# Experts by couples of pairs, with the rest rows of the second product in four quarters of TensorE's array

## The chip, the cores and the metric

The kernel runs on one core of a Trainium2 chip. The metric is the device time of one execution in microseconds (us). TensorE does the matrix products and writes to PSUM banks; VectorE and ScalarE read PSUM; GpSimd (POOL) issues gathers; SyncE (SP) issues the other DMAs. The engines run beside each other and meet at semaphores.

## The reference, cut to what matters

Two layers of a network on 256 tokens of width 512: cross-attention on a context of 4096 rows, self-attention and a feed-forward part, then attention with memory, self-attention and a mixture of experts. The change touches only the last part, the mixture of experts:

```python
logits = x @ router_w.T                      # 256 tokens, 64 experts
wts, idx = top_k(softmax(logits), 8)         # 8 experts a token, weights normalised
# each expert gets up to C = 64 of its tokens (slots)
h = silu(einsum('ecd,efd->ecf', xg, w1)) * einsum('ecd,efd->ecf', xg, v1)    # F = 192
y = einsum('ecf,efd->ecd', h, w2)            # D = 512
out = zeros(T, D).at[tok].add(y[e, slot] * weight)
```

The first products are [64 slots x 512] by [512 x 384] (w1 and v1 side by side), the second [64 x 192] by [192 x 512], for each of 64 experts. All of it is in float32.

## The kernel before, in words

Experts go by pairs: 32 pairs of 2 experts of 64 slots, so that a pair has 128 slot rows. The part begins when the tokens are routed, at about 1477 us. For a pair p:

- `up(p)` (L1912): for each of 4 chunks of the width, one product for each expert, with 64 stationary columns, that writes to its half of the partitions of a bank; the two use the array's column halves (L1924). 384 moving columns each.
- ScalarE applies Silu (L2028). `make_hid` (L2068) on VectorE multiplies by the other half and by the gate weight, into `h`: one instruction for hidden rows 0 to 127 and two for the rest, rows 128 to 191 (`REST` = 64), which go to different column blocks for the two experts, beside zeros.
- `turn(p)` (L1929): two transposes of `h` into `TURN_B`; `move_hid` (L2085) copies 256 columns to `hidT`.
- `down(p)` (L1938): two half-array products with hidden rows 0 to 127 of each expert (L1944), then one of the full array (L1945). Its 128 contraction rows are rows 128 to 191 of the first expert and rows 128 to 191 of the second; each expert's slots see zeros where the other's rows are.
- `round_y` on ScalarE (L2004) and `split_y` on VectorE (L2091) make a rounded part and a remainder of y. `make_selT` (L2058) makes a 0/1 matrix from slots to tokens.
- `spread_out(p)` (L1947): four products that add y into the 256 tokens' sums in two banks (L1953).

The order on TensorE is written out by hand: up(p), every fourth time `find_gates` (L1888, L41), `turn_rows(p+1)` (L1905, L1909), down(p-1), spread_out(p-2), turn(p). ScalarE and VectorE follow the same order with their parts. For pairs from 4 on, the tokens' rows are gathered from DRAM by POOL (`gpsimd_rows`, L1849), as soon as `move_gates` (L2047) has written the group's indices, into four buffers that `turn_rows` frees; a group is 4 pairs.

The weights of a pair are one DMA of 2304 KB (`w_moe`), issued by SP. There are 7 buffers (`N_RING`). The first 7 loads are issued at 1402 to 1406 us (L1855). Load p goes out when `down(p-7)` is finished:

```python
for p in range(N_RING, PAIRS):
    e.wait_ge(hid_down, p - N_RING + 1)
    e.dma_start(ring[p % N_RING][:], a["w_moe"][p]).then_inc(moe_in[p % N_RING], 16)
```

Of the kernel before, what the change touches and what calls it, by code (L numbers as in the profile page):

```python
# [6 lines left out]
F32 = mybir.dt.float32  # L7
# [3 lines left out]
ALU = mybir.AluOpType  # L11
# [3 lines left out]
P = 128  # L15
T, D = 256, 512
# [47 lines left out]
def build(nc, a, out):  # L64
    ctx = ExitStack()
    with ctx:
# [35 lines left out]

        IDENT_SET, ATT_SET, LOW_ONES, MASKS_SET, SLOTS_COUNTED, SLOTS_SET, H_ZEROED, IDS_COUNTED, IDS_SET = 4, (8, 9), 10, 12, 15, 17, 18, 19, 20

# [1657 lines left out]
        def gpsimd_memory(e):  # L1762
# [6 lines left out]
        N_RING, EPP, GROUP, FIRST, N_ROWS = 7, 2, 4, 4, 4  # L1769
        NG = PAIRS // GROUP  # L1770
        UPW = DT * 2 * FF
        W2 = EPP * UPW
# [9 lines left out]
            ("rows6", [P, N_ROWS, D], F32), ("xgT", [P, 2, DT, P], F32),  # L1782
            ("sa", [P, 2, FF], F32), ("h", [P, 2, 2 * P], F32), ("hidT", [P, 2, 2 * P], F32), ("gs", [P, 2, GROUP], F32),
            ("y_hi", [P, 2, D], F32R), ("y_lo", [P, 2, D], F32R), ("selT", [P, 2, T], F32R),
# [34 lines left out]
        PART = 3 * EPP  # L1819

        def gpsimd_slots(e):

            e.memset(low[:], 1.0).then_inc(consts_set, 1)
            e.memset(ones_m[:], 1.0).then_inc(consts_set, 1)
            e.wait_ge(consts_set, LOW_ONES)
            e.affine_select(out=low[:], in_=low[:], compare_op=ALU.is_gt, fill=0.0, base=0,
                            pattern=[[1, P]], channel_multiplier=-1).then_inc(consts_set, 1)
            e.iota(slot_row_i[:], pattern=[[1, CAP]], base=1, channel_multiplier=0).then_inc(consts_set, 1)
            for n, rows in enumerate(halves):
                e.wait_ge(consts_set, MASKS_SET + n + 1)  # L1830
                e.iota(slot_col_i[rows], pattern=[[0, 1]], base=1, channel_multiplier=1).then_inc(consts_set, 1)
            e.wait_ge(consts_set, SLOTS_COUNTED)
            e.tensor_copy(slot_row[:], slot_row_i[:]).then_inc(consts_set, 1)
            e.tensor_copy(slot_col[:], slot_col_i[:]).then_inc(consts_set, 1)
            e.memset(h[:], 0.0).then_inc(consts_set, 1)
            e.iota(ids_i[:], pattern=[[P, TT], [0, PAIRS], [0, EPP]], base=0, channel_multiplier=1).then_inc(consts_set, 1)
            e.wait_ge(consts_set, IDS_COUNTED)
            e.tensor_copy(gate_parts[:, :, :, 2 * EPP:], ids_i[:]).then_inc(consts_set, 1)
# [20 lines left out]
        def sync_moe(e):  # L1859
# [11 lines left out]
            for p in range(N_RING, PAIRS):  # L1871
                e.wait_ge(hid_down, p - N_RING + 1)
                e.dma_start(ring[p % N_RING][:], a["w_moe"][p]).then_inc(moe_in[p % N_RING], 16)
# [5 lines left out]
        def tensor_moe(e):  # L1879
# [8 lines left out]
            def find_gates(g):  # L1888

                e.wait_ge(sel_made, TT * (g + 1))  # L1890
                if g == 0:
                    e.wait_ge(route_gate, TT)
                    e.wait_ge(slot_moved, 1)
                    e.wait_ge(consts_set, IDS_SET)
                else:
                    e.wait_ge(gates_moved, 3 * g)
                    if g > 1:
                        e.wait_ge(hid_moved, GROUP * (g - 1))
                for n in range(GROUP):
                    pair = slice(n * P, (n + 1) * P)  # L1900
                    t = matmuls(e, TURN_B[:, 2 * P + PART * n:2 * P + PART * (n + 1)],
                                [(sel[:, g % 2, i, pair], gate_parts[:, i, GROUP * g + n, :]) for i in range(TT)])
                t.then_inc(gates_found, 1)

            def turn_rows(p):  # L1905
                e.wait_ge(*rows_landed(p))
                e.wait_ge(xg_moved, DT + p - GROUP)
                for c in range(DT):
                    t = e.transpose(GATHER_B[:, c * P:(c + 1) * P], rows6[:, p % N_ROWS, c * P:(c + 1) * P], ident[:])  # L1909
                t.then_inc(rows_turned, 1)  # L1910

            def up(p):  # L1912
                g, n = divmod(p, GROUP)
                e.wait_ge(moe_in[p % N_RING], 16 * (p // N_RING + 1))
                if p >= 2:
                    e.wait_ge(hid_made, 3 * (p - 1))
                if p >= GROUP:
# [10 lines left out]

            def turn(p):  # L1929
                e.wait_ge(hid_made, 3 * (p + 1))  # L1930
                if p:
                    e.wait_ge(hid_moved, p)
                e.wait_ge(gates_moved, 3 * min(p // GROUP + 2, NG))
                for n in range(2):
                    t = e.transpose(TURN_B[:, n * P:(n + 1) * P], h[:, p % 2, n * P:(n + 1) * P], ident[:])
                t.then_inc(hid_turned, 1)

            def down(p):  # L1938
                w2 = ring[p % N_RING]
                e.wait_ge(hid_moved, p + 1)  # L1940
                if p >= 2:
                    e.wait_ge(y_split, p - 1)
                for s, rows in enumerate(halves):
                    e.matmul(banks[Y_BANK[p % 2]][rows], hidT[:, p % 2, rows], w2[:, W2 + s * D:W2 + (s + 1) * D], start=True, stop=False)  # L1944
                e.matmul(banks[Y_BANK[p % 2]][:], hidT[:, p % 2, P:2 * P], w2[:, W2 + 2 * D:], start=False, stop=True).then_inc(hid_down, 1)  # L1945

# [30 lines left out]
            find_gates(0)  # L1977
            for p in range(PAIRS + 2):
                g, n = divmod(p, GROUP)
                if p < PAIRS:  # L1980
                    up(p)
                if n == 0 and g + 1 < NG:
                    find_gates(g + 1)
                if GROUP <= p + 1 < PAIRS:
                    turn_rows(p + 1)
                if 1 <= p <= PAIRS:
                    down(p - 1)
                if p >= 2:
                    spread_out(p - 2)
                if p < PAIRS:  # L1990
                    turn(p)

        def scalar_moe(e):
# [10 lines left out]
            def round_y(p):  # L2004
                e.wait_ge(hid_down, p + 1)
                if p >= 2:
# [13 lines left out]
            for c in range(DT):  # L2020
                move_xg(c)
            for p in range(PAIRS + 1):
                g, n = divmod(p, GROUP)
                if p < PAIRS:
                    e.wait_ge(hid_up, p + 1)
                    if p >= 2:
                        e.wait_ge(hid_made, 3 * (p - 1))
                    e.activation(sa[:, p % 2, :], banks[UP_BANKS[p % 2]][:, 0:FF], ACT.Silu).then_inc(hid_silu, 1)  # L2028
                if GROUP <= p + 1 < PAIRS:
                    move_rows(p + 1)  # L2030
                if p:
                    round_y(p - 1)

        def vector_moe(e):
# [12 lines left out]
            def move_gates(g):  # L2047
                e.wait_ge(gates_found, g + 1)
                if g >= 2:
                    e.wait_ge(hid_made, 3 * GROUP * (g - 1))  # L2050
                if g >= 3:
                    e.wait_ge(rows_turned, GROUP * (g - 2))
                found = TURN_B[:, 2 * P:2 * P + PART * GROUP].rearrange("p (n k) -> p n k", k=PART)
                e.tensor_copy(ids[:, g % 2, :], found[:, :, 2 * EPP]).then_inc(gates_moved, 1)
# [13 lines left out]
            def make_hid(p):  # L2068
# [3 lines left out]
                if n == 0:  # L2072
                    e.wait_ge(gates_moved, 3 * (g + 1))
                if p == 0:
                    e.wait_ge(consts_set, H_ZEROED)
                if p >= 2:
                    e.wait_ge(hid_turned, p - 1)
                e.wait_ge(hid_silu, p + 1)
                e.scalar_tensor_tensor(h[:, p % 2, 0:P], up_b[:, FF:FF + P], gs[:, g % 2, n:n + 1], sa[:, p % 2, 0:P],
                                       ALU.mult, ALU.mult).then_inc(hid_made, 1)  # L2080
                for s, rows in enumerate(halves):
                    e.scalar_tensor_tensor(h[rows, p % 2, P + s * REST:P + (s + 1) * REST], up_b[rows, FF + P:2 * FF],
                                           gs[rows, g % 2, n:n + 1], sa[rows, p % 2, P:FF], ALU.mult, ALU.mult).then_inc(hid_made, 1)

            def move_hid(p):  # L2085
                e.wait_ge(hid_turned, p + 1)
                if p >= 2:
                    e.wait_ge(hid_down, p - 1)
                e.tensor_copy(hidT[:, p % 2, :], TURN_B[:, 0:2 * P]).then_inc(hid_moved, 1)

# [40 lines left out]
            make_sel(1)  # L2131
            for p in range(PAIRS + 1):
                g, n = divmod(p, GROUP)
                if p < PAIRS:
                    make_hid(p)
                if n == 0 and g + 1 < NG:
                    move_gates(g + 1)
                if p:
                    split_y(p - 1)
                if p < PAIRS:  # L2140
                    move_hid(p)
                    if n == 1 and g + 2 < NG:
                        make_sel(g + 2)
                    make_selT(p)
            e.wait_ge(spread, PAIRS)
# [102 lines left out]
```

## Time and profile before

| | |
|---|---|
| median of 3 runs | 1696.14 us (1693.32 to 1700.35) |
| the profiled execution | 1698.13 us, its span 1696.3 us |
| TensorE's mean granted clock | 0.992 |
| busy: PE / PEld / DVE / ACT / POOL | 97% / 76% / 64% / 41% / 7% of the span |
| HBM read and written | 200.69 MB and 68.19 MB |
| weight loads of the experts | 32 of 2304 KB |

PE is TensorE's matmuls, PEld its loads of the stationary operand, DVE is VectorE, ACT ScalarE. The time of an execution is a little more than the span from its first to its last instruction. Lines such as L1945 are lines of the kernel before. One float32 matmul of the program stands in the trace as two MATMUL instructions.

### The profile page before, as it was taken

The page shows a single profiled execution, that of the slowest core. Times are in us where ns is not written, and L with a number is a line of the kernel's source. Part 1 is how long each engine was busy: PE and PEld are TensorE (multiplying, and loading weights), DVE is VectorE, ACT ScalarE, POOL GpSimd, SP SyncE. Part 2 cuts the span into 40 slices and gives each one's busy share as a digit, 9 for nine tenths or more (in the row PEclk, how much of TensorE's full clock was granted, in tenths as well). Part 3 has the DMA queues.
Part 4 walks back from the last instruction along what each step waited for, and adds up shares of the span by engine and source line. Part 5 has one row for each costly group of instructions (what it writes and reads, how often), then busy time and mean ns, then how long its engine had stood idle before and what let it go on. Part 6 is the DMA issues. An engine that isn't in the chain of part 4 may idle for free.

```text
span 1696.3 us, 23514 instructions
## 1 busy us (share of the span) xinstructions
PE 1651.4 (97%) x9232; PEld 1296.9 (76%) x9232; DVE 1089.0 (64%) x1754; ACT 696.2 (41%) x938; POOL 127.0 (7%) x213
## 2 busy tenths in 40 slices
PE   8998999999999999999999999998899999999998
PEld 7887888888788888888888888887657646644444
DVE  4445777777767777677777779997544923633333
ACT  3334444454444444445454456564321312222221
POOL 0000000000000000000000011101000000111110
PEclk9999999999999999999999999999889999999999
DMA  6755454455455445545545453326110529199991
GB/s 223 207 173 154 131 133 134 119 137 131 137 137 136 128 120 134 149 119 142 131 127 136 117 143 100 103 91 211 76 50 1 198 71 423 50 386 395 398 383 43
DMA packets 117293, 270.41 MB, mean 159 GB/s; under 512 B 7168, under 2 KB 76992, under 8 KB 111040
## 3 DMA queue, kind: packets, MB, share of 16 engines
q1 hardware_dynamic: 96512, 194.45, 36.5%
q0 software_dynamic: 20672, 74.46, 14.9%
q8 instruction: 74, 1.21, 0.3%
q14 instruction: 35, 0.29, 0.1%
HBM read 200.69 MB, written 68.19 MB: 159 GB/s over the span
## 4 chain that ended last, share of the span: by engine, by line
PE 77%; issue 11%; DVE 5%; DMA 3%; ACT 2%; POOL 1%; SPq 0%; DVEq 0%; POOLq 0%; ACTq 0%
PE bank L390 18%; PE bank L41 17%; PE bank L362 14%; PE bank L403 7%; PE bank L1924 5%; PE bank L1554 3%; PE bank L1945 2%; PE bank L1944 2%; DMA v_dram<-v_out 2%; PE bank L1953 2%; PE bank L135 2%; PE bank L428 1%; PE bank L1909 1%; DVE e_lo L719 1%; DMA v_out<-in_wv 1%
## 5 line engine op out<-in xcount | busy, mean ns | idle before, releaser
L719 DVE TENSOR_TENSOR e_lo<-S,e_hi 128x1024 fp32r<-128x1024 f32 x128 | 156.6, 1224 | 90.3 <-ACT e_hi L548 89.8
L362 PE MATMUL bank<-cT_hi,wk_hi 128*128 128x512 f32 x512 | 205.4, 401 | 0.0
L390 PE MATMUL bank<-wv_hi,cT_hi 128*128 128x512 f32 x512 | 200.0, 391 | 3.5 <-DVE wv_lo L656 3.5
L539 ACT ACTIVATE S<-S 128x1024 f32<-128x1024 f32 x128 | 135.8, 1061 | 158.5 <-DVE S L699 158.0
L362 PE MATMUL bank<-cT_hi,wk_lo 128*128 128x512 f32 x512 | 200.5, 392 | 0.0
L390 PE MATMUL bank<-wv_hi,cT_lo 128*128 128x512 f32 x512 | 199.4, 389 | 0.0
L390 PE MATMUL bank<-wv_lo,cT_hi 128*128 128x512 f32 x512 | 199.2, 389 | 0.0
L362 PE MATMUL bank<-cT_lo,wk_hi 128*128 128x512 f32 x512 | 199.2, 389 | 0.0
L548 ACT CAST e_hi<-S 128x1024 fp32r<-128x1024 f32 x128 | 134.8, 1053 | 141.3 <-PE bank L403 136.7
L712 DVE TENSOR_TENSOR esum<-esum,S 128x512 f32<-128x512 f32 x210 | 145.0, 690 | 71.2 <-ACT S L539 67.6
L403 PE MATMUL bank<-e_hi,v_back 128*128 128x256 f32 x880 | 168.5, 289 | 6.3 <-DVE e_lo L719 3.9
L687 DVE TENSOR_TENSOR mx<-mx,S 128x512 f32<-128x512 f32 x224 | 154.3, 689 | 14.3 <-ACT S L533 10.4
L699 DVE TENSOR_TENSOR S<-S,mrow 128x1024 f32<-128x1024 f32 x128 | 155.4, 1216 | 3.2 <-POOL mrow L896 3.2
L41 PE MATMUL bank<-q_hi,k_hi 128*128 128x256 f32 x512 | 145.3, 284 | 9.3 <-DVE k_lo L674 9.3
L403 PEld LDWEIGHTS bank<-e_hi,v_back 128*128 128x128 f32 x880 | 139.5, 193 | 11.2 <-DMA v_back<-v_dram 5.1
L41 PE MATMUL bank<-q_lo,k_hi 128*128 128x256 f32 x512 | 144.8, 283 | 0.0
L41 PE MATMUL bank<-q_hi,k_lo 128*128 128x256 f32 x512 | 144.8, 283 | 0.0
L519 ACT CAST k_hi<-bank 128x512 fp32r<-128x512 f32 x128 | 75.3, 588 | 155.3 <-PE bank L362 155.3
L533 ACT COPY S<-bank 128x1024 f32<-128x1024 f32 x128 | 128.7, 1006 | 11.1 <-PE bank L41 11.1
L403 PE MATMUL bank<-e_lo,v_back 128*128 128x256 f32 x440 | 124.9, 284 | 0.0
L890 POOL DMA_DIRECT2D v_back<-v_dram x110 | 59.0, 537 | 870.2 <-PE bank L403 833.9
L724 DVE TENSOR_TENSOR v_out<-bank,v_out 128x512 fp32r<-128x512 f32 x112 | 76.9, 687 | 60.3 <-ACT v_out L555 60.3
(280 smaller groups left out, 2872.2 us busy)
## 6 DMA issues: line engine op xcount, KB each, us to landing
w<-in_w_moe SPq DMA_DIRECT2D x32, 2304.0 KB, 11.6
v_dram<-v_out SPq DMA_DIRECT2D x112, 512.0 KB, 4.5
v_back<-v_dram POOLq DMA_DIRECT2D x110, 512.0 KB, 5.0
v_dram<-v_back SPq DMA_DIRECT2D x16, 512.0 KB, 3.9
ctx_nat<-in_ctx SPq DMA_DIRECT2D x8, 1024.0 KB, 5.2
ctx_raw<-in_ctxT SPq DMA_DIRECT2D x7, 1024.0 KB, 7.8
v_late<-v_dram POOLq DMA_DIRECT2D x14, 512.0 KB, 3.6
l_w_qkv<-in_l_wqkv SPq DMA_DIRECT2D x6, 1024.0 KB, 5.6
```

Source lines behind the costliest of these rows:

```text
L41: last = e.matmul(dst, lhs, rhs, start=(n == 0), stop=(n == len(terms) - 1))
L362: t = e.matmul(banks[b][:], l, r, start=(c == 0 and m == 0), stop=(c == DT - 1 and m == 2))
L390: t = e.matmul(banks[b][:], l, r, start=(c == 0 and m == 0), stop=(c == DT - 1 and m == 2))
L403: t = e.matmul(banks[O_BANK][:, 0:T], v[:, i, l, :], r[:, i, :], start=(j == 0 and i == 0 and m == 0), stop=(j == NCH - 1 and i == CT - 1 ...
L533: e.copy(S[:, j * CT:(j + 1) * CT, :].rearrange("p a t -> p (a t)"), twin[:]).then_inc(s_stored, 1)
L539: e.activation(Sj, Sj, ACT.Exp).then_inc(raised, 1)
L548: e.copy(e_place(n)[0][:], S[:, j * CT:(j + 1) * CT, :]).then_inc(e_rounded, 1)
L687: own.done(e.tensor_tensor(mx[:], mx[:], two, ALU.max))
L699: e.tensor_tensor(Sj, Sj, mrow[:].unsqueeze(1).to_broadcast([P, CT, T]), ALU.subtract).then_inc(shifted, 1)
L712: e.tensor_tensor(esum[:], esum[:], two, ALU.add).then_inc(e_summed, 1)
L719: e.tensor_tensor(lo[:], Sj, hi[:].bitcast(F32), ALU.subtract).then_inc(e_split, 1)
L1924: t = e.matmul(banks[UP_BANKS[p % 2]][rows, 0:2 * FF], inputs[:, s * P // 2:(s + 1) * P // 2], ring[p % N_RING][:, s * UPW + c * 2 * FF:s ...
```

## The change

Two pairs, a couple, go through each step together: 16 couples q of pairs 2q and 2q+1. The order on TensorE is up(2q), on every second couple find_gates, up(2q+1), turn_rows(2q+2), down of couple q-1, spread_out of both pairs of couple q-2, turn(q), turn_rows(2q+3).

`h` has 384 columns: 128 main columns of the first pair, 128 of the second, then 64 rest columns of the first and 64 of the second. The two experts of a pair share columns now, so that no zeros are needed, and one transpose puts the first pair's rest rows on partitions 0 to 63 and the second pair's on 64 to 127. In `down`, the four main products come first, then four products of 64 contraction rows and 64 stationary columns, one for each quarter of the array: rows of the array by pair, columns by expert; each pair adds to its own bank. The host lays the rest of `w2` out to fit. The loads' sizes stay the same. SP waits for whole couples: loads p = 2q+5 and 2q+6 need `down` of couple q-1. The gates of groups from 1 on are found in `GATHER_B`, which `turn_rows` uses too, and not in `TURN_B`.

```diff
+            return (TURN_B[:, 2 * P:2 * P + PART * GROUP] if g == 0 else GATHER_B[:, 0:PART * GROUP]).rearrange("p (n k) -> p n k", k=PART)
...
-            e.memset(h[:], 0.0).then_inc(consts_set, 1)
...
-                e.wait_ge(hid_down, p - N_RING + 1)
+                e.wait_ge(hid_down, (p - N_RING) // 2 + 1)
...
+                if p % GROUP == 2 and p // GROUP + 1 < NG:
+                    e.wait_ge(gates_moved, 3 * (p // GROUP + 2))
...
+            def turn(q):
+
+                e.wait_ge(hid_made, 4 * (q + 1))
+                if q:
+                    e.wait_ge(hid_moved, q)
+                else:
+                    e.wait_ge(gates_moved, 3)
+                for n in range(3):
+                    t = e.transpose(TURN_B[:, n * P:(n + 1) * P], h[:, n * P:(n + 1) * P], ident[:])
+                t.then_inc(hid_turned, 1)
+
+            def down(q):
+
+                e.wait_ge(hid_moved, q + 1)
+                if q:
+                    e.wait_ge(y_split, 2 * q)
+                ring_of = [ring[(2 * q + n) % N_RING] for n in range(2)]
                 for n in range(2):
-                    t = e.transpose(TURN_B[:, n * P:(n + 1) * P], h[:, p % 2, n * P:(n + 1) * P], ident[:])
-                t.then_inc(hid_turned, 1)
-
-            def down(p):
-                w2 = ring[p % N_RING]
-                e.wait_ge(hid_moved, p + 1)
-                if p >= 2:
-                    e.wait_ge(y_split, p - 1)
+                    for s, rows in enumerate(halves):
+                        e.matmul(banks[Y_BANK[n]][rows], hidT[:, n * P + s * P // 2:n * P + (s + 1) * P // 2],
+                                 ring_of[n][:, W2 + s * D:W2 + (s + 1) * D], start=True, stop=False)
                 for s, rows in enumerate(halves):
-                    e.matmul(banks[Y_BANK[p % 2]][rows], hidT[:, p % 2, rows], w2[:, W2 + s * D:W2 + (s + 1) * D], start=True, stop=False)
-                e.matmul(banks[Y_BANK[p % 2]][:], hidT[:, p % 2, P:2 * P], w2[:, W2 + 2 * D:], start=False, stop=True).then_inc(hid_down, 1)
+                    for n, rest in enumerate(halves):
+                        t = e.matmul(banks[Y_BANK[n]][rows], hidT[rest, 2 * P + s * P // 2:2 * P + (s + 1) * P // 2],
+                                     ring_of[s][rest, W2 + 2 * D:], start=False, stop=True)
+                t.then_inc(hid_down, 1)
...
+            for q in range(COUPLES + 2):
+                if q < COUPLES:
+                    up(2 * q)
+                    if q % 2 == 0 and q // 2 + 1 < NG:
+                        find_gates(q // 2 + 1)
+                    up(2 * q + 1)
+                if GROUP <= 2 * q + 2 < PAIRS:
+                    turn_rows(2 * q + 2)
+                if 1 <= q <= COUPLES:
+                    down(q - 1)
+                if q >= 2:
+                    spread_out(2 * q - 4)
+                    spread_out(2 * q - 3)
+                if q < COUPLES:
+                    turn(q)
+                if GROUP <= 2 * q + 3 < PAIRS:
+                    turn_rows(2 * q + 3)
...
-                for s, rows in enumerate(halves):
-                    e.scalar_tensor_tensor(h[rows, p % 2, P + s * REST:P + (s + 1) * REST], up_b[rows, FF + P:2 * FF],
-                                           gs[rows, g % 2, n:n + 1], sa[rows, p % 2, P:FF], ALU.mult, ALU.mult).then_inc(hid_made, 1)
...
+                e.scalar_tensor_tensor(h[:, rest:rest + REST], up_b[:, FF + P:2 * FF], gs[:, g % 2, n:n + 1], sa[:, p % 2, P:FF],
+                                       ALU.mult, ALU.mult).then_inc(hid_made, 1)
+
+            def move_hid(q):
+                e.wait_ge(hid_turned, q + 1)
+                if q:
+                    e.wait_ge(hid_down, q)
+                e.tensor_copy(hidT[:], TURN_B[:, 0:3 * P]).then_inc(hid_moved, 1)
...
+            for q in range(COUPLES + 1):
+                if q < COUPLES:
+                    if q % 2 == 0 and q // 2 + 1 < NG:
+                        move_gates(q // 2 + 1)
+                    make_hid(2 * q)
+                    make_hid(2 * q + 1)
+                if q:
+                    for p in (2 * q - 2, 2 * q - 1):
+                        split_y(p)
+                        make_selT(p)
+                if q < COUPLES:
+                    move_hid(q)
+                    if q % 2 and q // 2 + 2 < NG:
+                        make_sel(q // 2 + 2)
```

## Rows read from the trace of the kernel before

**Rows 1.** Busy time by stretches: PE, PEld, DVE, ACT, POOL, clock, DMA, GB/s.
```profile
1500.00:1656.00 156.00, 156.00 (x790) 74.96 (x788) 57.30 (x168) 34.61 (x69) 22.77 (x24) 1.00 0.99 398
1500.00:1530.00 30.00, 30.00 (x158) 14.45 (x155) 10.57 (x32) 6.35 (x13) 3.80 (x4) 1.00 1.01 427
...
1560.00:1600.00 40.00, 40.00 (x201) 18.91 (x201) 15.45 (x43) 9.03 (x18) 6.64 (x7) 1.00 0.98 375
```

**Rows 2.** Chain of waits, pairs 4 and 5: start us, us, what.
```profile
1499.65 2.73 PE bank L1924 x16
1502.38 0.98 PE bank L41 x8
1503.37 0.52 PE bank L1909 x4
1503.88 1.01 PE bank L1944 x4
1504.89 1.06 PE bank L1945 x2
1505.95 0.92 PE bank L1953 x4
...
1507.09 2.73 PE bank L1924 x16
1509.82 0.59 PE bank L1909 x4
...
1513.62 0.47 PE bank L1924
```

**Rows 3.** Chain of waits at the start of the expert part.
```profile
1477.35 2.75 PE bank L1924 x16
...
1482.06 0.41 PE bank L1935 x2
...
1485.20 0.86 PE bank L1944 x4
```

**Rows 4.** Chain of waits from the last pair's first products on.
```profile
1681.35 2.73 PE bank L1924 x16
...
1691.27 1.21 PE bank L1953 x4
```

**Rows 5.** Chain of waits in self-attention, then that line's instructions by shape.
```profile
1430.51 0.43 PE bank L1062 x8
...
L1062 PE MATMUL bank<-l_qkT x64: 372/374/478, 1429.7 to 1450.3; 32*128 32x256 f32 x64
```

**Rows 6.** Weight loads: issue and landing of two, landing of the last.
```profile
L1873 SPq DMA_DIRECT2D w<-in_w_moe x1: 339/339/339, 1492.0 to 1492.0; - x1
...
DMA to landing us min/median/max: 14.4/14.4/14.4
...
L1873 SPq DMA_DIRECT2D w<-in_w_moe x1: 328/328/328, 1525.6 to 1525.6; - x1
...
DMA to landing us min/median/max: 11.2/11.2/11.2
...
DMA to landing us min/median/max: 12.2/12.2/12.2
```

**Rows 7.** Groups of 1476 to 1697 us on ScalarE and VectorE: busy, mean ns, idle.
```profile
L2095 DVE TENSOR_TENSOR y_lo<-bank,y_hi 128x512 fp32r<-128x512 f32 x32 | 22.1, 692 | 64.0 <-ACT y_hi L2008 64.0
L2008 ACT CAST y_hi<-bank 128x512 fp32r<-128x512 f32 x32 | 18.8, 586 | 49.4 <-PE bank L1945 49.4
...
L2089 DVE COPY hidT<-bank 128x256 f32<-128x256 f32 x32 | 13.3, 415 | 0.6 <-PE bank L1935 0.6
...
L2066 DVE TENSOR_SCALAR selT<-slot_all,slot_col 128x256 fp32r<-128x256 bf16 x32 | 11.1, 345 | 0.0
```

**Rows 8.** Gathers of token rows: issues and landings of all 28.
```profile
L1849 POOL DMA_INDIRECT rows<-xn_dram,ids x28: 947/947/1189, 1483.0 to 1652.3; - x28
...
DMA to landing us min/median/max: 4.1/8.9/13.3
```

More of the change, by code:

```diff
@@ L100, in build @@
         own = Steps(vector_step)
-        IDENT_SET, ATT_SET, LOW_ONES, MASKS_SET, SLOTS_COUNTED, SLOTS_SET, H_ZEROED, IDS_COUNTED, IDS_SET = 4, (8, 9), 10, 12, 15, 17, 18, 19, 20
+        IDENT_SET, ATT_SET, LOW_ONES, MASKS_SET, SLOTS_COUNTED, SLOTS_SET, IDS_COUNTED, IDS_SET = 4, (8, 9), 10, 12, 15, 17, 18, 19
         def gpsimd_constants(e):
@@ L1770, in build @@
         NG = PAIRS // GROUP
+        COUPLES = PAIRS // 2
         UPW = DT * 2 * FF
@@ L1782, in build @@
             ("rows6", [P, N_ROWS, D], F32), ("xgT", [P, 2, DT, P], F32),
-            ("sa", [P, 2, FF], F32), ("h", [P, 2, 2 * P], F32), ("hidT", [P, 2, 2 * P], F32), ("gs", [P, 2, GROUP], F32),
+            ("sa", [P, 2, FF], F32), ("h", [P, 3 * P], F32), ("hidT", [P, 3 * P], F32), ("gs", [P, 2, GROUP], F32),
             ("y_hi", [P, 2, D], F32R), ("y_lo", [P, 2, D], F32R), ("selT", [P, 2, T], F32R),
@@ L1819, in build, with gates_place @@
         PART = 3 * EPP
+        def gates_place(g):
+            return (TURN_B[:, 2 * P:2 * P + PART * GROUP] if g == 0 else GATHER_B[:, 0:PART * GROUP]).rearrange("p (n k) -> p n k", k=PART)
         def gpsimd_slots(e):
@@ L1896, in find_gates @@
                     e.wait_ge(gates_moved, 3 * g)
-                    if g > 1:
-                        e.wait_ge(hid_moved, GROUP * (g - 1))
+                    e.wait_ge(xg_moved, DT + GROUP * (g - 2) + 2 if g > 1 else DT)
                 for n in range(GROUP):
                     pair = slice(n * P, (n + 1) * P)
-                    t = matmuls(e, TURN_B[:, 2 * P + PART * n:2 * P + PART * (n + 1)],
+                    t = matmuls(e, gates_place(g)[:, n, :],
                                 [(sel[:, g % 2, i, pair], gate_parts[:, i, GROUP * g + n, :]) for i in range(TT)])
@@ L1915, in up @@
                 if p >= 2:
-                    e.wait_ge(hid_made, 3 * (p - 1))
+                    e.wait_ge(hid_made, 2 * (p - 1))
                 if p >= GROUP:
@@ L1927, in up @@
                 t.then_inc(hid_up, 1)
[L1929 to L1933, printed above, removed]
-                for n in range(2):
-                    t = e.transpose(TURN_B[:, n * P:(n + 1) * P], h[:, p % 2, n * P:(n + 1) * P], ident[:])
-                t.then_inc(hid_turned, 1)
-            def down(p):
-                w2 = ring[p % N_RING]
-                e.wait_ge(hid_moved, p + 1)
-                if p >= 2:
-                    e.wait_ge(y_split, p - 1)
+            def turn(q):
[12 more added lines that the diff above has]
+                ring_of = [ring[(2 * q + n) % N_RING] for n in range(2)]
+                for n in range(2):
+                    for s, rows in enumerate(halves):
+                        e.matmul(banks[Y_BANK[n]][rows], hidT[:, n * P + s * P // 2:n * P + (s + 1) * P // 2],
+                                 ring_of[n][:, W2 + s * D:W2 + (s + 1) * D], start=True, stop=False)
                 for s, rows in enumerate(halves):
-                    e.matmul(banks[Y_BANK[p % 2]][rows], hidT[:, p % 2, rows], w2[:, W2 + s * D:W2 + (s + 1) * D], start=True, stop=False)
-                e.matmul(banks[Y_BANK[p % 2]][:], hidT[:, p % 2, P:2 * P], w2[:, W2 + 2 * D:], start=False, stop=True).then_inc(hid_down, 1)
+                    for n, rest in enumerate(halves):
+                        t = e.matmul(banks[Y_BANK[n]][rows], hidT[rest, 2 * P + s * P // 2:2 * P + (s + 1) * P // 2],
+                                     ring_of[s][rest, W2 + 2 * D:], start=False, stop=True)
+                t.then_inc(hid_down, 1)
             def spread_out(p):
@@ L1977, in tensor_moe @@
             find_gates(0)
[L1978 to L1991, printed above, removed]
+            for q in range(COUPLES + 2):
[15 more added lines that the diff above has]
+                    turn_rows(2 * q + 3)
         def scalar_moe(e):
@@ L2004, in round_y @@
             def round_y(p):
-                e.wait_ge(hid_down, p + 1)
+                e.wait_ge(hid_down, p // 2 + 1)
                 if p >= 2:
@@ L2021, in scalar_moe @@
                 move_xg(c)
[L2022 to L2032, printed above, removed]
+            for q in range(COUPLES + 1):
+                if q < COUPLES:
+                    for p in (2 * q, 2 * q + 1):
+                        e.wait_ge(hid_up, p + 1)
+                        if p >= 2:
+                            e.wait_ge(hid_made, 2 * (p - 1))
+                        e.activation(sa[:, p % 2, :], banks[UP_BANKS[p % 2]][:, 0:FF], ACT.Silu).then_inc(hid_silu, 1)
+                if GROUP <= 2 * q + 2 < PAIRS:
+                    move_rows(2 * q + 2)
+                if q:
+                    round_y(2 * q - 2)
+                    round_y(2 * q - 1)
+                if GROUP <= 2 * q + 3 < PAIRS:
+                    move_rows(2 * q + 3)
         def vector_moe(e):
@@ L2049, in move_gates @@
                 if g >= 2:
-                    e.wait_ge(hid_made, 3 * GROUP * (g - 1))
+                    e.wait_ge(hid_made, 2 * GROUP * (g - 1))
                 if g >= 3:
                     e.wait_ge(rows_turned, GROUP * (g - 2))
-                found = TURN_B[:, 2 * P:2 * P + PART * GROUP].rearrange("p (n k) -> p n k", k=PART)
+                found = gates_place(g)
                 e.tensor_copy(ids[:, g % 2, :], found[:, :, 2 * EPP]).then_inc(gates_moved, 1)
@@ L2073, in make_hid @@
                     e.wait_ge(gates_moved, 3 * (g + 1))
-                if p == 0:
-                    e.wait_ge(consts_set, H_ZEROED)
                 if p >= 2:
-                    e.wait_ge(hid_turned, p - 1)
+                    e.wait_ge(hid_turned, p // 2)
                 e.wait_ge(hid_silu, p + 1)
-                e.scalar_tensor_tensor(h[:, p % 2, 0:P], up_b[:, FF:FF + P], gs[:, g % 2, n:n + 1], sa[:, p % 2, 0:P],
+                main, rest = p % 2 * P, 2 * P + p % 2 * REST
+                e.scalar_tensor_tensor(h[:, main:main + P], up_b[:, FF:FF + P], gs[:, g % 2, n:n + 1], sa[:, p % 2, 0:P],
                                        ALU.mult, ALU.mult).then_inc(hid_made, 1)
-                for s, rows in enumerate(halves):
-                    e.scalar_tensor_tensor(h[rows, p % 2, P + s * REST:P + (s + 1) * REST], up_b[rows, FF + P:2 * FF],
-                                           gs[rows, g % 2, n:n + 1], sa[rows, p % 2, P:FF], ALU.mult, ALU.mult).then_inc(hid_made, 1)
[L2085 to L2089, printed above, removed]
+                e.scalar_tensor_tensor(h[:, rest:rest + REST], up_b[:, FF + P:2 * FF], gs[:, g % 2, n:n + 1], sa[:, p % 2, P:FF],
[5 more added lines that the diff above has]
+                e.tensor_copy(hidT[:], TURN_B[:, 0:3 * P]).then_inc(hid_moved, 1)
             def split_y(p):
@@ L2131, in vector_moe @@
             make_sel(1)
[L2132 to L2144, printed above, removed]
+            for q in range(COUPLES + 1):
+                if q < COUPLES:
[3 more added lines that the diff above has]
+                    make_hid(2 * q + 1)
+                if q:
+                    for p in (2 * q - 2, 2 * q - 1):
+                        split_y(p)
+                        make_selT(p)
+                if q < COUPLES:
+                    move_hid(q)
+                    if q % 2 and q // 2 + 2 < NG:
+                        make_sel(q // 2 + 2)
             e.wait_ge(spread, PAIRS)
@@ L2221 @@
     w2_main = w2[:, :P].reshape(PAIRS, 2, P, D).transpose(0, 2, 1, 3)
-    moe = (up.reshape(PAIRS, P, -1), w2_main.reshape(PAIRS, P, -1), w2[:, P:].reshape(PAIRS, P, D))
+    moe = (up.reshape(PAIRS, P, -1), w2_main.reshape(PAIRS, P, -1), w2[:, P:].reshape(PAIRS // 2, 2, 2, P // 2, D).transpose(0, 2, 1, 3, 4).reshape(PAIRS, P, D))
     laid = {
```

## The prediction

> **What bounds the kernel now.** I read the busy table by stretches first. In the last stage (1477 to 1692 us) TensorE is busy for all of every stretch at clock 1.00, while VectorE is busy for under half; the DMA share stands near 1 as well [rows 1]. So two resources are near their limit, and I read both. The chain of waits, in order of time, shows TensorE alone from 1499.65 on: no piece of another engine lies between its pieces [rows 2]. A pair takes 6.53 us (1507.09 to 1513.62), and one in four, with the gate search (L41, 0.98), takes 7.44 (1499.65 to 1507.09). Four pairs take 3 x 6.53 + 7.44 = 27.03 us. Weights for later pairs land 11 to 14 us after their issue [rows 6] and are first needed six pairs later, so today they are never waited for.
>
> **How TensorE's pieces are priced.** The two half products of `down` (L1944) take 1.01 us behind transposes of the full array, but 0.86 directly behind `up`, which uses the array in halves too [rows 2, 3]: so 0.86 is the streaming and 0.15 the change from the one use of the array to the other. The third product (L1945, full array, half of its stationary matrix zeros) is 1.06, again 0.86 and 0.20 for the change. `up` is 2.73 behind a full-array piece, so I take 2.58 behind another `up`. `turn_rows` (L1909) is 0.59 behind `up`, 0.52 behind a full-array piece. A `spread_out` (L1953) is 0.92, and the last 0.22 of a pair are the two transposes of `turn`, 0.11 each.
>
> **The change, part by part.**
>
> 1. The rest products. Two full products (2.12 us with their changes) become one group of four quarters per couple. No row shows a 64 by 64 quarter. Nearest from below: four products of 32 rows each, each to a bank of its own, take 0.43 us for 256 columns, the streaming time of a single one (half the 0.86 of 512 columns) [rows 2, 5]; and two halves by columns stream in the time of one [rows 3]. If both compose, four quarters of 512 columns take 0.86. I add 0.14 for a new use of the array: 1.00. Bounds: 0.86 if the change costs nothing; 4 x 0.86 = 3.44 if no two overlap.
>
> 2. The main products of the two pairs stand one behind the other: 1.01 + 0.86 = 1.87 (was 2.02).
>
> 3. Both spreads stand behind the quarters: 2 x 0.92 and the change back, 0.15: 2.00 (was 1.84).
>
> 4. Three transposes for four: 0.33. The `turn_rows` of the odd pair now follows them: 0.52 for 0.59.
>
> A couple without gate search: 2.73 + 2.58 + 0.59 + 1.87 + 1.00 + 2.00 + 0.33 + 0.52 = 11.62. With it, 0.98 more and 0.15 because the second `up` is behind it: 12.75. Four pairs: 24.37 for 27.03, which is 2.66 less.
>
> Edits with no price: VectorE makes h in 2 instructions for 3 and copies 384 columns once for twice 256; ScalarE's work is unchanged. Both lie beside TensorE, and VectorE gets lighter. The memset on POOL goes, long before its reader. Queued behind something new is `move_hid`: it stands behind the y of the previous couple, which ScalarE rounds only after spread 2q-3. That is 0.59 + 0.69 + 0.35 and some 0.6 for the copy (384 columns for 256's 0.42), 2.2 us after the spreads in all [rows 7], and `down` needs it 7 us later, behind turn, turn_rows and two `up`s. Covered; but not at the end (below). The new wait of `turn_rows` on the gates is met during the 2.73 us of `up`. The gathered rows have less lead: the first gather of a group is issued by POOL some 4.9 us into the couple with the gate search (2.73 + 0.98, and 1.2 for the indices on VectorE and the semaphores) and needed 12.75 + 5.3 = 18.1 us in, so 13.2 us for landings of 4.1 to 13.3, median 8.9 [rows 8]. Covered, but for the longest.
>
> **Start.** Today `up` starts at 1477.35 (pair 0) and 1499.65 (pair 4). Now: up 0 to 1480.08, gates to 1481.06, up 1 to 1483.79; Silu and two products of VectorE for h, 1.2 us (today three of them put the first turn 1.98 us behind up 0, 1480.08 to 1482.06 [rows 3]), turn to 1485.45; up 2 and up 3 to 1490.76. The rows of pair 4 are gathered from 1483.0 on (0.3 earlier now) and land 8.9 us later at the median [rows 8], at 1491.6: a stall of 0.8 before turn_rows, which ends at 1492.2; down 0 to 1495.1, turn and turn_rows to 1496.1. Pair 4 starts 3.5 us earlier than today.
>
> **Middle.** Couples 2 to 13, six of either kind: 6 x (12.75 + 11.62) = 146.2, to 1642.3. Couple 14, without gates, 11.62: to 1653.9. `up` of pair 31 starts at 1653.9 + 2.73 = 1656.6 (today 1681.35 [rows 4]) and ends at 1659.2, 24.9 earlier than today's 1684.08.
>
> **End.** Today 8.4 us from there to the end of the last spread (1692.48) [rows 4]. Now a whole couple has to be finished with no `up` to lie beside: down 14 (2.72), spreads (2.0), the y of pair 29 ahead of the last hidT (2.3 with its semaphores), down 15 (3.0), spreads 28 and 29 (2.0), then round, split, selT and spread of pair 31 with pair 30's between (3.0): 15.0. Given back: 6.6.
>
> **Sum.** -24.9 + 6.6 = -18.3 us. The profiled execution took 1698.13 us around its span of 1696.3, 2 us above the median of the three runs, 1696.14; I take the difference from the median: 1677.8, rounded 1678.
>
> **Does DMA keep up?** A pair needs 2304 KB of weights and 256 KB of rows, 2.62 MB. At 27.03 us for four pairs that is 388 GB/s; at 24.37 it is 430. What the stage has shown: 427 GB/s from 1500 to 1530, when loads were queued up. Their landings went from 1492.0 + 14.4 to 1525.6 + 11.2, five loads later [rows 6]: 6.08 us each, just the 6.09 that TensorE will ask for. But from 1560 to 1600 the share is 0.98 with 375 GB/s, and over 1500 to 1656 it is 0.99 with 398 [rows 1]: either the engines were full and slower (6.59 us a pair), or the share counts waiting packets and 388 was simply all that was asked. The landings do not grow there (the last of all is 12.2 [rows 6]), which favours the second. Slots also come free later, and by twos: first at 1495.1 (end of down 0). The first load then lands by 1506.3 to 1509.5 (11.2 to 14.4 us), and 24 more must land by 1656.6: there are 6.13 to 6.26 us for each. At 6.08 no load is late; at 6.59 the last is late by 7.9 to 11 us.
>
> The Trainium skill (DMA: Bandwidth & Descriptors, section Where 436 GB/s comes from) says that HBM binds such loads at about 358 GB/s per core. An estimate by that figure is 7.3 us a pair and thus rival E below. The trace does not agree: 427 GB/s over 30 us, and 398 over 156 [rows 1]. The skill (TensorE: Matmul & The Clock Gate, section Measured speedup vs the span model) gives 3.07x for four tiles by rows; by that the quarters would take 3.44 / 3.07 = 1.12 us, not 1.00, and the sum would be 1680. Here four such products took the time of one [rows 5].
>
> **Rivals.**
>
> A. *DMA becomes the bound*: 6.59 us a pair; 1678 + 8 to 11 = 1686 to 1689. For it: share near 1 already. Against it: 427 GB/s with loads queued up. Chance 0.20.
>
> B. *Quarters overlap only in twos*, by columns: 1.72 + 0.14 for 1.00, 16 times, +13.8: 1692. Against it: row tiles overlap four at a time [rows 5]. 0.08.
>
> C. *Gathered rows come late*, because weights are loaded by twos: each microsecond beyond 13.2 costs 7 us over the seven groups; with 2 us late, 1692. Against it: half of them land within 8.9 [rows 8]. 0.05.
>
> D. *The other side: the quarters run one behind another.* 3.44 + 0.14 for 1.00, 16 times, +41: 1719. The change breaks even when the group of quarters takes 1.00 + 18.3/16 = 2.14 us, and is slower by over 0.5% from 2.67. Against it: both kinds of overlap are in the trace, though never together. 0.06.
>
> E. *DMA held well below what this trace reached*: a pace a fifth slower than the 6.08 of the rows, 7.3 us a pair, would land the last load at 1506.3 + 24 x 7.3 = 1681.5, 25 us late: 1703. Against it: no busy stretch here is that slow [rows 1]. 0.01.
>
> The remaining 0.60 is the forecast. Its own range: quarters at 0.86 and free changes of use (-0.3 a couple) give 1673; quarters at 1.12 and a stall of 2 us give 1682. About 0.5% (8.5 us) is what a measurement of this kernel can tell from no change. The range 1673 to 1690 holds forecast and A, 0.8. Faster than 1687.7: the forecast and most of A, 0.79; within 0.5%: the rest of A, B, C and E, 0.15; slower, D: 0.06.
>
> **What would show it.** Four pairs from `up` to `up` in 24.4 us; the quarters' piece 1.0 us in the chain (1.86 would be B, 3.6 D); TensorE without idle time in the middle. Idle time before `up` released by a weight DMA is A, before `turn_rows` released by the gather is C. The first weight issue near 1495, `up` of pair 31 near 1657, and 15 us from its end to the last spread. The prediction is wrong if the quarters do not overlap or if loads at full queue take over 6.3 us a pair.

## The result, and the profile of the changed kernel

The changed kernel takes 1678.25 us (median of 4 runs, 1675.72 to 1682.86), the kernel before 1695.85 in the same comparison; the ratio is 0.9893, interval 0.9877 to 0.9908. The prediction said 1678, range 1673 to 1690. The two medians differ by 17.6 us.

The profiled executions differ by more, 1698.13 and 1675.72 us. The 4.8 us beyond those 17.6 are not the change's. In the profile after, the first `up` starts at 1472.51 and not at 1477.35 [rows 3], and nothing ahead of it was changed. In later profiles of kernels with the same stages ahead it starts at 1474 to 1479. So the comparison that bears on the change is the expert part alone, from the first `up` to the end of the last spread: 215.1 us before (1477.35 to 1692.48 [rows 3, 4]), 197.6 after (1472.51 to 1670.08). That is 17.6 less, and 18.3 was forecast.

The chain of waits of the changed kernel, couples 3 and 4 (start us, us, what):

```profile
1504.57 0.44 PE bank L1915 x4
1505.01 5.31 PE bank L1930 x32
1510.32 0.59 PE bank L1915 x4
1510.90 1.87 PE bank L1954 x8
1512.77 1.02 PE bank L1958 x8
1513.79 2.04 PE bank L1968 x8
1515.83 0.33 PE bank L1943 x3
1516.16 0.44 PE bank L1915 x4
1516.59 2.73 PE bank L1930 x16
1519.32 0.98 PE bank L41 x8
1520.31 2.73 PE bank L1930 x16
...
1529.33 0.79 PE bank L1930 x3
```

L1930 is `up`, L1954 the main products, L1958 the quarters, L1968 the spreads, L1943 and L1915 the transposes. Beside [rows 2]: the couple without gate search takes 11.58 us (1505.01 to 1516.59), the one with it 12.74 (1516.59 to 1529.33), so four pairs take 24.32 for 27.03. The quarters of two pairs take 1.02 us where two full products took 2.12.

The same view at the start and at the end of the expert part:

```profile
1472.51 2.73 PE bank L1930 x16
1475.24 1.00 PE bank L41 x8
...
1477.74 9.39 DMA rows<-xn_dram,ids
1487.13 0.04 issue
1487.17 0.66 PE bank L1915 x4
1487.83 1.87 PE bank L1954 x8
...
1493.68 1.21 DVE sel L2064 x2
1494.90 0.04 issue
1494.94 1.05 PE bank L41 x8
...
1649.81 5.31 PE bank L1930 x32
...
1661.58 0.48 DVE hidT L2108
1662.05 0.04 issue
1662.10 1.94 PE bank L1954 x8
...
1667.99 2.09 PE bank L1968 x8
```

TensorE waits at four places of this chain: for the first gathered rows, at the second gate search, which needs `sel`, at the last `down`, which needs `hidT`, and at the last spread, which needs `selT`. The waits of TensorE in the expert part, all of them over 0.5 us (waiter, releaser: total, times, longest):

```profile
PE bank L1954 <- DVE hidT L2108: 1.9, 1, 1.9
...
PE bank L1915 <- DMA rows<-xn_dram,ids: 1.4, 1, 1.4
...
PE bank L1943 <- DVE h L2101: 1.0, 1, 1.0
PE bank L1968 <- DVE selT L2087: 0.9, 1, 0.9
...
PE bank L41 <- DVE sel L2064: 0.6, 1, 0.6
```

The fifth wait, for `h`, is that of the first transposes and lies beside the gather. None of them is for a weight load. But the stretches show how near that is (columns as in [rows 1]):

```profile
1530.00:1560.00 30.00, 30.00 (x180) 14.50 (x178) 10.22 (x29) 7.09 (x15) 4.35 (x5) 1.00 1.01 423
1560.00:1600.00 40.00, 40.00 (x236) 19.41 (x233) 13.46 (x37) 9.20 (x19) 6.63 (x7) 1.00 1.01 423
1600.00:1640.00 40.00, 40.00 (x235) 20.26 (x235) 14.21 (x37) 10.78 (x21) 4.74 (x5) 1.00 1.01 424
```

The last load was issued at 1635.5 and landed 14.9 us later:

```profile
L1878 SPq DMA_DIRECT2D w<-in_w_moe x25: 327/334/538, 1490.8 to 1635.5; - x25
...
DMA to landing us min/median/max: 14.9/14.9/14.9
```

That is 1650.4. Its `up` (pair 31) begins at 1649.81 + 2.65 = 1652.5. So DMA comes out of 24 loads at its full rate only 2 us ahead of TensorE.

### The profile page after: what moved, and what is told of

Read it like the earlier page. It is cut to its first block, busy times and chain, and to the rows that moved or that the text cites. A ratio compares the mean times of both kernels' runs of the same rounds, so it can differ in the third digit from the quotient of the medians.

```text
span 1673.9 us, 23515 instructions
## 1 busy us (share of the span) xinstructions
PE 1624.5 (97%) x9280; PEld 1285.7 (77%) x9280; DVE 1076.1 (64%) x1706; ACT 695.1 (42%) x938; POOL 127.0 (8%) x212
## 4 chain that ended last, share of the span: by engine, by line
PE 71%; issue 16%; DVE 6%; DMA 3%; ACT 2%; POOL 2%; SPq 0%; DVEq 0%; POOLq 0%; ACTq 0%
PE bank L390 16%; PE bank L41 16%; PE bank L362 12%; PE bank L403 7%; PE bank L1930 4%; PE bank L1554 3%; PE bank L1968 2%; PE bank L1954 2%; DMA v_dram<-v_out 1%; DVE e_lo L719 1%; PE bank L135 1%; PE bank L428 1%; PE bank L1958 1%; POOL v_back L890 1%; PE bank L1915 1%
## 5 line engine op out<-in xcount | busy, mean ns | idle before, releaser
L362 PE MATMUL bank<-cT_lo,wk_hi 128*128 128x512 f32 x512 | 199.2, 389 | 0.0
L390 PE MATMUL bank<-wv_lo,cT_hi 128*128 128x512 f32 x512 | 199.2, 389 | 0.0
## 6 DMA issues: line engine op xcount, KB each, us to landing
w<-in_w_moe SPq DMA_DIRECT2D x32, 2304.0 KB, 17.5
```

What stands on the lines that cost most here:

```text
L362: t = e.matmul(banks[b][:], l, r, start=(c == 0 and m == 0), stop=(c == DT - 1 and m == 2))
L390: t = e.matmul(banks[b][:], l, r, start=(c == 0 and m == 0), stop=(c == DT - 1 and m == 2))
```

## The experiments

The first three change only the rest products of the changed kernel's `down`, to price an overlap by taking it away. "Expert part" below is always from the first `up` to the end of the last spread, in the profiled execution; the changed kernel's was 197.6, 199.2 and 197.4 us in three profiles.

### Two products of the full array for the quarters

```diff
-                for s, rows in enumerate(halves):
-                    for n, rest in enumerate(halves):
-                        t = e.matmul(banks[Y_BANK[n]][rows], hidT[rest, 2 * P + s * P // 2:2 * P + (s + 1) * P // 2],
-                                     ring_of[s][rest, W2 + 2 * D:], start=False, stop=True)
+                for n in range(2):
+                    t = e.matmul(banks[Y_BANK[n]][:], hidT[:, 2 * P:3 * P], ring_of[n][:, W2 + 2 * D:], start=False, stop=True)
```

> The changed kernel, but the four quarters of a couple are replaced by two products of the full array, one into each bank (all 128 rows of rest against one pair's rest weights, so y is not the reference's). Same order, same loads, same waits. My theory (the quarters stream together, and a change of the array's use costs 0.15 to 0.20 us): this group takes 0.20 + 2 x 0.86 = 1.93 us for 1.02, and the spreads behind it 1.86 for 2.04; 0.73 us more a couple, 16 couples, +11.7: about 1690 us. If the gain came from the new order alone and the quarters cost as much as full products, it stays at 1678.

Measured: 1688.8 us, 0.9954 of before (0.9937 to 0.9972). Expert part 1474.60 to 1683.53, 208.9 us: 11.4 more than the changed kernel's, 11.7 expected. Its chain:

```profile
1567.88 1.91 PE bank L1957 x4
1569.80 1.85 PE bank L1966 x8
```

The group takes 1.91 for 1.02, and the spreads, which now stand behind a group that uses the full array too, 1.85 for 2.04. So of the 17.6 us that the change won, some 11.4 are the quarters'; the other 6 are the new order's, after the 6.6 us that it costs at the end.

### All four on the same rows of the array

```diff
-                        t = e.matmul(banks[Y_BANK[n]][rows], hidT[rest, 2 * P + s * P // 2:2 * P + (s + 1) * P // 2],
-                                     ring_of[s][rest, W2 + 2 * D:], start=False, stop=True)
+                        t = e.matmul(banks[Y_BANK[n]][rows], hidT[halves[0], 2 * P + s * P // 2:2 * P + (s + 1) * P // 2],
+                                     ring_of[s][halves[0], W2 + 2 * D:], start=False, stop=True)
```

The loop over n also went outside the loop over s.

> The changed kernel, but all four quarter products use array rows 0 to 63 (rest rows of the first pair for both banks, so y is not the reference's). Two can overlap by columns, none by rows. My theory: overlap by rows is real, and taking it away adds one streaming time, 0.86 us a couple, +13.8: about 1692 us, the group 1.88 us. Rival B of the prediction (overlap by columns only, all along): no change, 1678.

Measured: 1692.55 us, 0.9968 of before (0.9956 to 0.9981); expert part 1475.73 to 1686.57, 210.8 us, 13.3 more. The group:

```profile
1569.49 1.86 PE bank L1958 x8
```

1.86 is 2 x 0.86 and 0.14, one streaming time more than 1.02, less a little. The overlap by rows is real, and rival B is out.

### All four in one quarter

```diff
-                        t = e.matmul(banks[Y_BANK[n]][rows], hidT[rest, 2 * P + s * P // 2:2 * P + (s + 1) * P // 2],
-                                     ring_of[s][rest, W2 + 2 * D:], start=False, stop=True)
+                        t = e.matmul(banks[Y_BANK[n]][halves[0]], hidT[halves[0], 2 * P + s * P // 2:2 * P + (s + 1) * P // 2],
+                                     ring_of[s][halves[0], W2 + 2 * D:], start=False, stop=(s == 1))
```

The main products of the other half end their sums themselves (stop).

> The changed kernel, but all four rest products use the same quarter of the array and write to partitions 0 to 63 (so y is not the reference's). Nothing can overlap: 4 x 0.86 + 0.15 = 3.6 us for 1.02, 16 times, +41: about 1719 us, slower than before. If each product of 64 x 64 were cheaper than a full one (a quarter of the work), it would stay near 1678.

Measured: 1719.96 us, 1.0133 of before (1.0116 to 1.015); expert part 238.3 us (1475.03 to 1713.33), 40.7 more, 41 expected.

```profile
1565.00 3.58 PE bank L1958 x8
```

3.58 is 4 x 0.86 and 0.14. A product of a quarter of the array costs as much time as one of the whole; all that the smaller shape gives is that three others can run beside it. This is rival D's price, and it would have made the kernel slower.

### An earlier last turn

```diff
-                if q:
+                if 0 < q < COUPLES - 1:
                     e.wait_ge(y_split, 2 * q)
+                y_banks = last_y_banks if q == COUPLES - 1 else Y_BANK      # last_y_banks = UP_BANKS
...
                     down(q - 1)
+                if q == COUPLES - 1:
+                    turn(q)
...
                     make_hid(2 * q + 1)
+                if q == COUPLES - 1:
+                    move_hid(q)
```

The later calls of `turn` and `move_hid` are left out for the last couple, and `round_y` and `split_y` read the other banks for pairs 30 and 31.

> The changed kernel with another end: the last couple's transposes come directly behind down of couple 14, its hidT is copied ahead of the y of the previous couple, and its down writes to the two banks that up has left, so that it waits for no y. The output is the reference's. My theory: the 2.2 us in which TensorE waits between the spreads and the last down go, about 2 us less: 1676 us, below what the times can tell, so the chain decides: down of couple 15 should begin some 5.1 us after the last up and not 7.0. A rival: the wait only moves to the y of pairs 28 and 29 before their spreads, and nothing is won.

Measured: 1678.83 us, 0.9887 of before (0.987 to 0.9903), which the times do not tell from the changed kernel's 0.9893. The chain:

```profile
1654.41 5.31 PE bank L1934 x32
1659.72 1.72 PE bank L1959 x8
1661.44 1.02 PE bank L1963 x8
1662.46 0.48 PE bank L1947 x3
1662.93 1.85 PE bank L1973 x8
1664.79 1.87 PE bank L1959 x8
```

The last `down` begins 5.07 us after the last `up` and not 6.98 (1655.12 to 1662.10). The spreads follow without a wait, so the rival is out. Expert part 195.7 us (1477.04 to 1672.72). The same kernel a second time, with the changed kernel beside it:

> The kernel with the early last turn once more, beside the changed kernel on one chip. Its profile had no idle time before the last down, while the changed kernel's waited 1.9 us there, and in one of its two profiles the granted clock then fell to 0.5 and that down took 3.6 us for 1.9. My theory: 2 us less always and 1.7 more where the clock falls, so 2 to 4 us less than the changed kernel, its last down 1.87 us. A rival: the upstream stages differ by more than that from run to run, and the medians show nothing.

> The changed kernel, for comparison with the run before: ratio to before 0.989. In its profile the last down stands behind 1.9 us of idle time, at 1.9 us if the clock holds and 3.6 if it falls.

Measured: 1676.36 us, 0.9874 (0.9858 to 0.9891), against 1679.68 us, 0.9887 (0.987 to 0.9903) on the same chip. Expert parts 195.4 and 197.4 us. The profiles show the 2 us both times. The medians, 3.3 us apart, point the same way, but their intervals overlap, so the times alone do not tell it. The clock had not fallen in either of these two profiles, so the further 1.7 us that was expected where it falls is not shown.

### Less work for TensorE, before and after

Both leave out the two products with `y_lo` in each `spread_out`, in the one the kernel before, in the other the changed kernel:

```diff
-                    for part in (y_hi, y_lo):
-                        t = e.matmul(banks[OUT_BANKS[i]][:], selT[:, p % 2, i * P:(i + 1) * P], part[:, p % 2, :],
-                                     start=(p == 0 and part is y_hi), stop=(p == PAIRS - 1 and part is y_lo))
+                    t = e.matmul(banks[OUT_BANKS[i]][:], selT[:, p % 2, i * P:(i + 1) * P], y_hi[:, p % 2, :],
+                                 start=(p == 0), stop=(p == PAIRS - 1))
```

> The kernel before, with the two products of y's remainder left out of every spread_out (the result loses its low part). TensorE's pair falls by 2 x 0.23 = 0.46 us, four pairs to 25.2 us, that is 416 GB/s of weights and rows asked for. My theory: TensorE alone bounds the kernel before, and DMA can give 424, so all of 32 x 0.46 = 14.8 us is won: ratio 0.9913, some 1681 us on a chip where before takes 1696. A rival, that DMA was the bound already (398 GB/s over the stage): little is won.

> The changed kernel with the same products left out. TensorE's four pairs would fall from 24.35 to 22.5 us, 466 GB/s asked for. My theory: the changed kernel stands within 2 us of DMA's limit (the last load landed at 1650.4, its up began at 1652.5, and from 1510 to 1640 the engines moved 419 to 431 GB/s in every 10 us), so that up of the last pair comes only some 2 us earlier, and the spreads after it save 1.8: 4 us, about 1674, with TensorE waiting before up some 10 us in all. A rival: DMA has room, and again 14.8 us are won, 1663.5.

Measured on one chip, where before takes 1698.13 us and the changed kernel 1680.22 (0.9892, 0.9875 to 0.9908):

| | without the low products | won |
|---|---|---|
| before | 1685.02 us, 0.992 (0.9904 to 0.9937) | 13.1 us |
| changed | 1676.68 us, 0.987 (0.9854 to 0.9887) | 3.5 us |

The same 14.8 us of TensorE's work is worth 13 us before the change and about 3.5 after it. The intervals of the changed kernel with and without the products overlap, so the 3.5 is not exact; its expert part is 3.9 us shorter (195.3 for 199.2). That it is far less than 14.8 is clear. In the first run the pair in the chain is 6.07 us for 6.53:

```profile
1606.56 2.73 PE bank L1924 x16
...
1612.62 2.73 PE bank L1924 x16
```

Its second `up` took 4.43 us for 2.73, at a granted clock of 0.51 from 1481 to 1483, so this profile lost 1.7 us there:

```profile
1480.93 4.43 PE bank L1924 x16
```

DMA followed; from 1560 to 1600:

```profile
1560.00:1600.00 40.00, 40.00 (x202) 17.98 (x200) 16.19 (x45) 9.76 (x20) 5.50 (x6) 1.00 1.00 416
```

So the 375 GB/s at a share of 0.98 that the kernel before had in the same 40 us [rows 1] was what it asked for, not what DMA could give. In the second the same line, and the waits:

```profile
1560.00:1600.00 40.00, 37.49 (x223) 17.24 (x221) 13.89 (x39) 9.63 (x20) 6.48 (x7) 1.00 1.01 422
```

```profile
PEld bank L1930 <- DMA w<-in_w_moe: 10.5, 8, 2.6
PE bank L1930 <- DMA w<-in_w_moe: 6.8, 6, 1.9
```

PEld and PE are two sides of the same waits. Now `up` waits for weights: its matmuls six times, 6.8 us in all (some 10 were expected), while DMA moves 422 GB/s, no more than in the changed kernel. This is the mechanism of rival A, DMA as the bound, seen once TensorE is made quicker still. Its pace is not rival A's: 2.62 MB at 422 GB/s are 6.2 us a pair, not 6.59.

### The same with smaller loads

```diff
-                e.dma_start(ring[p % N_RING][:], a["w_moe"][p]).then_inc(moe_in[p % N_RING], 16)
+                e.dma_start(ring[p % N_RING][:, :W2], a["w_moe"][p][:, :W2]).then_inc(moe_in[p % N_RING], 16)
```

> As the run before (no products of y's remainder), and from load 7 on only the first-product weights are loaded, 1536 KB of 2304 (the second products use the weights that lie there from the first loads, so y is not the reference's). TensorE's work is the same; DMA's falls to some 4.4 us a pair. My theory: the wait goes and TensorE bounds it again: 14.8 us less than the changed kernel, 1663.5. If what held the run before were the release of buffers in twos, or the gathers' lead, and not the rate of DMA, it stays with that run.

Measured: 1667.75 us, 0.9831 (0.9814 to 0.9847): 12.5 us below the changed kernel, 9 below the run with whole loads. No wait for weights is left, and DMA moves 308 GB/s over 1500 to 1640. The order, the releases by twos and the gathers were the same, so it was what DMA had to move that held the run before. It is 2.3 us short of the 14.8 expected. The waits name most of that, small ones on VectorE (0.6 and 0.9 us in the changed kernel) that now come to the front:

```profile
PE bank L41 <- DVE sel L2063: 2.0, 6, 0.6
...
PE bank L1967 <- DVE selT L2086: 1.5, 2, 1.3
```

### The changed kernel again

> The changed kernel once more, on the chip of these runs, to compare the others with: ratio to before 0.989, expert part some 17.5 us shorter than before's.

Measured: 1680.22 us, ratio as above. Expert part 199.2 us (1476.09 to 1675.26), 15.9 shorter than before's and not 17.5. The missing 1.6 us are one piece at the end, the last `down`:

```profile
1665.59 3.61 PE bank L1954 x8
```

The stretches around it (columns as in [rows 1]):

```profile
1664.00:1666.00 2.00, 0.41 (x2) 0.22 (x4) 1.53 (x4) 0.09 (x1) 0.00 (x0) 0.93 0.00 0
1666.00:1668.00 2.00, 2.00 (x6) 0.48 (x4) 0.00 (x0) 0.00 (x0) 0.00 (x0) 0.50 0.00 0
1668.00:1670.00 2.00, 2.00 (x12) 0.21 (x8) 0.00 (x0) 0.00 (x0) 0.00 (x0) 0.72 0.00 0
```

After the idle time before this `down` the granted clock stood at 0.50, the lower level of 1.2 GHz, and the products took 3.61 us for 1.94.

## Why the prediction was right

By its own terms, in us:

| term | forecast | measured |
|---|---|---|
| the quarters of a couple | 1.00 | 1.02 |
| main products, spreads | 1.87, 2.00 | 1.87, 2.04 |
| both `up`s without, with gate search between | 5.31, 6.44 | 5.31, 6.44 |
| turn and `turn_rows` of the odd pair | 0.33, 0.52 | 0.33, 0.44 |
| four pairs | 24.37 | 24.32 |
| start: first `up` to `up` of pair 4 (1491.6) | 18.8 | 19.1 |
| middle: from there to `up` of pair 30 | 157.8 | 158.2 |
| end: from the end of the last `up` to that of the last spread | 15.0 | 14.96 |
| expert part against before | -18.3 | -17.6 |

**The quarters.** The step with the least ground was that overlap by rows and overlap by columns compose, when the trace before had each only by itself. The profile shows 1.02 us. Without the overlap by rows it is 1.86, without either 3.58, and two full products take 1.91: all as worked out from the one streaming time of 0.86. That rules out rivals B and D. The estimate of 1.12 us that the prediction set beside its 1.00 has no change of use in it; like for like it would have been 1.26.

**The price of changing the array's use.** Read as 0.15 to 0.20 us from two places of one trace, it held at the new borders: 1.02 for the quarters is 0.86 and 0.16, and the spreads behind them take 2.04, 0.19 more than the 1.85 behind full products. Where no border stands, the price is not paid: the second `up` takes 2.58, the second pair's main products 0.86 (1.87 for two). One term was too dear, the odd pair's `turn_rows` behind `turn`: 0.44 and not 0.52; it outweighs the 0.02 and 0.04 by which the quarters and the spreads were too cheap. The Trainium skill (TensorEngine Tiling (Array Packing), section Key Properties) says that a change of the tiling mode drains TensorE; the 0.15 to 0.20 us here agree with it.

**The start** was off by 0.3 us: the first gathered rows kept TensorE waiting 1.4 us, and 0.8 was forecast. **The middle** has a wait that was not named, 0.6 us, once: the second gate search waits for `sel`, which VectorE makes behind `hidT` and the y of two pairs.

**The end** was the term of the order that costs, and it came as worked out: 2.74 for `down` of couple 14, 4.24 to the last `down`, 2.95 for it, 5.03 behind it. It need not be so long: the early last turn gets 2 us back in its profiles.

**DMA** (rivals A and E). That no load would be late was right, but by less than the prediction's 6.08 us a pair made it seem. That pace was read from two landings five loads apart, in a stretch of 427 GB/s. The changed kernel moves 423 to 425 GB/s in each stretch of 30 to 50 us between 1510 and 1640, an estimated 6.2 us a pair (2.62 MB at 423 GB/s), while TensorE uses up a pair in 6.08. So the lead of the loads shrinks through the stage, and 2 us of it are left at the last load. Neither rival's pace was seen, 6.59 (A) or 7.3 (E).

**Gathers** (rival C) were late only once, at the start, but the ground for its small chance, half of them landed within 8.9 us, did not last. The trace after shows a landing for 7 of the 28 gathers only, the fourth of each group: 8.7 to 13.1 us, median 11.8. In the trace before, the same seven have a median of 7.9 (7.6 to 13.3). The first gather of a group is the one that the 13.2 us are for. Its landing is not shown. The one issued at 1521.33 was needed by the `turn_rows` that began at 1534.64 without a wait, so it landed within 13.3 us, by an unknown margin.

The time was met to 0.3 us partly by luck: the expert part itself missed by 0.7 us, its start moves by some 6 us between profiles, and the medians even that out only in part.

## What to carry to other kernels

Products that use a part of TensorE's array cost as much time as full ones and pay only by what runs beside them: count the groups that can share a streaming time, and the borders between uses of the array. Before a piece of TensorE's work is taken out, work out what DMA would be asked for afterwards, and take its limit from a stretch in which loads were queued up; here the next 14.8 us of TensorE's work were worth about 3.5. Work in larger steps makes the end of the pipeline longer, and the end can be ordered by hand apart from the loop.

## What the runs showed of the hardware

The DMA share of a stretch does not tell a full DMA from one that keeps up. It was 0.98 at 375 and 0.99 at 398 GB/s [rows 1], when 388 was asked for, and 1.01 at 422 with `up` waiting; with the smaller loads it was still 0.82 at 308. What told them apart was the rate with loads queued up. The landings of weight loads point the same way, with medians of 11.2 us before, 14.9 after and 17.4 in the run with waits, but the last two are from the 7 and 4 loads of 25 whose landing the traces show, and loads go out by twos there.

TensorE's clock after a short idle time differs between profiles of the same kernel. Of eight profiles in which the last `down` came behind some 2 us of idle time, five show it at 1.94 us with the clock at 1.00, and three at 3.57 to 3.61 us with the clock at 0.50 in the two microseconds that lie wholly inside it. The two profiles with the early last turn, without that idle time, have 1.87. The falls go with the chip more plainly than with the kernel: all three are from the chip of the runs with less work for TensorE, and the fourth profile of that chip, the kernel before without the low products, has its fall in the second `up` (0.51), behind 1.0 us of idle time. Five profiles with that idle time at the end, four of them from two other chips, have none; nor have the two with the early last turn, which are from those two chips as well. So whether the early last turn keeps the clock up is not shown, and what decides is not settled by these runs.
